# Linear attention and gated linear attention on one core: another order of work in the second pass

## The reference

```
x = x + layernorm(attn(layernorm(x)))      # 16 heads of 32: relu(q), relu(k), linear attention
x = x + layernorm(ffn(layernorm(x)))       # 8 heads of 64: gated linear attention, 5 paths

# inside ffn, per tile of rows
q1, k1, v = x@Wq, x@Wk, x@Wv
q2 = x@Wqa@Wqb;  k2 = softmax(x@Wka@Wkb)
gk1, gk2 = log_sigmoid(x@Wg1a@Wg1b + bg1)/16, log_sigmoid(x@Wg2a@Wg2b + bg2)/16
e = softmax(x@We); one expert of 4 per row (top 1)
o  = chunk_gla(q1, k1, v, gk1) + sum over experts of chunk_gla(q2*e, k2*e, v, gk2*mask)
o  = o * rsqrt(mean(o*o) + eps) * norm_w * silu(x@Wga@Wgb)
return o @ Wo
```

## Time and profile before

| | us |
|---|---|
| median of 3 runs (3140.97 to 3148.92) | 3148.73 |
| the profiled execution | 3142.66 |
| its span, first to last instruction | 3140.8 |
| TensorE busy | 2876.9 (92%) |
| VectorE busy | 1962.6 (62%) |
| ScalarE busy | 1639.7 (52%) |
| GpSimd busy | 1355.5 (43%) |

### The profile page before, as it was taken

How to read it: one execution, slowest core, us unless ns; L and a number is a source line. 1 busy time by engine, 2 the same in 40 slices (tenths; PEclk the granted TensorE clock), 3 DMA queues, 4 the chain that set the end, 5 groups by cost and what they waited for, 6 DMA issues and landing times.

```text
span 3140.8 us, 56322 instructions
## 1 busy us (share of the span) xinstructions
PE 2876.9 (92%) x20720; PEld 1830.1 (58%) x20720; DVE 1962.6 (62%) x3878; ACT 1639.7 (52%) x3281; POOL 1355.5 (43%) x1006
## 2 busy tenths in 40 slices
PE   6999899999999999999879988999999999999997
PEld 3444566666666666666534445666666666666665
DVE  4442666667666676666544426666667666666675
ACT  4332555555555565555433325555556555555553
POOL 2873444444444444444322334444444444444443
PEclk9999999999999999999889999999999999999999
DMA  4121000000000000000021110000000000000000
GB/s 171 61 94 41 18 20 20 20 20 20 20 20 20 20 20 20 20 20 20 18 85 57 67 41 18 20 20 20 20 20 20 20 20 20 20 20 20 20 20 11
DMA packets 48376, 97.49 MB, mean 31 GB/s; under 512 B 5376, under 2 KB 5376, under 8 KB 47680
## 3 DMA queue, kind: packets, MB, share of 16 engines
q1 hardware_dynamic: 37008, 68.44, 6.5%
q10 hardware_dynamic: 9792, 17.83, 1.5%
q0 software_dynamic: 1520, 10.50, 0.8%
HBM read 63.19 MB, written 33.55 MB: 31 GB/s over the span
## 4 chain that ended last, share of the span: by engine, by line
PE 77%; DVE 16%; ACT 3%; issue 3%; POOL 1%; DVEq 0%; DMA 0%; POOLq 0%; SPq 0%; ACTq 0%
PE psum L303 12%; PE psum L448 11%; PE psum L304 11%; PE psum L305 11%; PE psum L547 5%; DVE region L1106 5%; PE psum L437 4%; PE psum L312 4%; PE psum L457 4%; PE psum L413 3%; DVE region L1090 3%; PE psum L353 2%; PE psum L423 2%; ACT ogT L730 2%; PE psum L352 2%
## 5 line engine op out<-in xcount | busy, mean ns | idle before, releaser
L977 POOL TENSOR_TENSOR region<-region,kfac 128x512 f32<-128x512 f32 x64 | 66.8, 1043 | 842.3 <-DVE kfac L1190 842.3
L448 PE MATMUL psum<-region 128*128 128x128 f32 x2560 | 352.2, 305 | 10.8 <-POOL region L959 10.8
L448 PEld LDWEIGHTS psum<-region 128*128 128x128 f32 x2560 | 346.1, 221 | 14.5 <-issue 11.1
L959 POOL TENSOR_TENSOR region<-region,mb 128x512 f32<-128x512 f32 x256 | 322.7, 1292 | 73.3 <-ACT region L620 72.9
L992 POOL TENSOR_TENSOR region<-region,decay 64x1280 f32<-64x1280 f32 x128 | 298.3, 2330 | 117.9 <-DVE decay L1206 112.9
L972 POOL TENSOR_SCALAR region<-region,m 128x512 f32<-128x512 f32 x256 | 172.9, 697 | 285.7 <-DVE hm L1141 210.5
L303 PE MATMUL psum<-wb,region 128*128 128x512 f16 x768 | 292.4, 381 | 3.3 <-DVE mb L1155 3.3
L304 PE MATMUL psum<-wb,region 128*128 128x512 f16 x768 | 292.0, 380 | 0.0
L305 PE MATMUL psum<-wb,region 128*128 128x512 f16 x768 | 291.7, 380 | 0.0
L951 POOL TENSOR_TENSOR region<-region 128x1024 f32<-128x1024 f32 x64 | 146.7, 2292 | 287.4 <-DVE region L1302 229.9
L1302 DVE SCALAR_TENSOR_TENSOR region<-psum,region 128x512 f16<-128x512 f32 x64 | 44.3, 692 | 261.0 <-ACT region L791 261.0
(11 more groups left out here) (233 smaller groups left out, 7580.7 us busy)
## 6 DMA issues: line engine op xcount, KB each, us to landing
region<-x_in SPq DMA_DIRECT2D x128, 256.0 KB, 2.7
q_cols<-region ACTq DMA_DIRECT2D x64, 256.0 KB, 2.4
region<-q_cols SPq DMA_DIRECT2D x64, 256.0 KB, 2.9
out_rows<-region SPq DMA_DIRECT2D x60, 256.0 KB, 2.0
region<-wb_in POOLq DMA_DIRECT2D x1, 3072.0 KB, 11.2
region<-wqkv_in SPq DMA_DIRECT2D x4, 512.0 KB, 6.2
region<-wqkv_in POOLq DMA_DIRECT2D x2, 1024.0 KB, 5.6
region<-wproj_in POOLq DMA_DIRECT2D x2, 1024.0 KB, 7.4
```

Of the source, the lines that this page charges most:

```text
L448: last = mm(bank[7][:, pr * P:(pr + 1) * P], q, state[:, pr, path, :], start=(pr == 0 and path == 0), stop=False, skip_group_check=True)
L959: last = nc.gpsimd.tensor_tensor(qm[:, e, :, :], q2T, mb[:, e, :].unsqueeze(1).to_broadcast([P, PAIRS, P]), ALU.mult)
```

## The change

Nothing is added or removed but one wait; pieces of `step` trade places on three engines. On TensorE `inter` and `intra` of the last tile stand between `project_v` and `gates`; `den` stands behind `project_q`; `out_mm` stands right behind `og_transpose`, ahead of `cumulate`; `half_sums` stands behind `y_mm`. Since `inter` writes bank 7, it now also waits for low0_ok of tile n, after which ScalarE has read the low-rank products. ScalarE and VectorE follow with their own pieces.

```diff
-            def inter(n):
+            def inter(n, front):
                 pe.wait_ge(S("out_ok"), prev(n))
+                if front:
+                    pe.wait_ge(S("low0_ok"), cur(n + 1))
                 pe.wait_ge(S("state_ok"), cur(n))
...
                 if front:
                     low_rank(n)
                     project_v(n)
+                if back:
+                    inter(m, front)
+                    intra(m, mp)
+                if front:
                     gates(n)
                     project_k2(n)
+                    label_bc(n)
+                    project_k(n)
+                    project_q(n)
                 if ahead:
                     den(n + 1, mp)
-                if front:
-                    label_bc(n)
-                if back:
-                    inter(m)
-                    intra(m, mp)
-                if front:
-                    project_k(n)
-                    project_q(n)
                 if back:
                     og_transpose(m)
+                    out_mm(m)
                 if front:
                     cumulate(n)
-                if back:
-                    out_mm(m)
-                if front:
-                    half_sums(n)
                 if ahead:
                     y_mm(n + 1)
                 if front:
+                    half_sums(n)
                     transposes(n)
...
# ScalarE
                     front_v(n, p)
+                    front_router(n)
+                if back:
+                    back_square(m)
+                if front:
                     front_gates(n, 0)
-                    front_router(n)
+                if back:
+                    back_rms(m)
+                if front:
                     front_gates(n, 1)
                     front_ke(n)
+                    front_sig_high(n)
+                    front_sig(n)
                 if ahead:
                     ahead_z(n + 1)
                 if back:
-                    back_square(m)
-                if front:
-                    front_sig_high(n)
-                if back:
-                    back_rms(m)
-                if front:
-                    front_sig(n)
-                if back:
                     back_og(m)
+                    back_norm3(m)
                 if front:
                     front_exps(n)
-                if back:
-                    back_norm3(m)
-                if front:
                     front_exs(n, p)
...
# VectorE
                     front_router(n)
+                if back:
+                    back_norm(m)
+                if front:
                     front_masks(n)
                     front_kmax(n)
                     front_kdiff(n)
-                    front_logsig(n)
-                if ahead:
-                    ahead_qz(n + 1, mp)
-                if back:
-                    back_norm(m)
-                if front:
-                    front_lslow(n)
                 if back:
                     back_normed(m, mp)
                     back_gated(m, mp)
                     back_split(m)
                 if front:
+                    front_logsig(n)
                     front_kfac(n)
+                    front_lslow(n)
                     front_sil(n, p)
                 if ahead:
+                    ahead_qz(n + 1, mp)
                     ahead_qz_split(n + 1)
```

## The result

The changed kernel takes 3356.19 us (median of 4 runs, 3356.14 to 3357.26), the kernel before 3147.64 (4 runs, 3140.97 to 3148.92): a ratio of 1.067, 95% interval 1.065 to 1.069. It is slower, as forecast, but by 209 us and not by 400: 3356 lies under the stated range of 3370 to 3660, and 9 us from the time that the prediction gave to its second rival (3347).

The account below looks back on a forecast made before the run. TensorE was taken as the bound, 77% of the chain of waits. Step 38.7 us, new pauses 8.0, removed 2.85, clock 3.3: 45.2, 6.5 longer; 62 steps give 403, first steps 4, forecast 3550 us, range 3370 to 3660.

Parts of the forecast that it names:

- second rival: New pauses come, but the clock stays up or falls lie inside pauses: step 41.9 us, 3347 in all; chance 0.10.
- What the change removes: TensorE's pause ahead of the gates goes, 2.43 us a step from start to start.
- The four new pauses: Places in a step where TensorE now comes too early: 8.0 us in sum, at full clock.
- (a): Project_k, now right behind the labels, waits for VectorE's masks: 1.65 us a step.
- (b): Project_q waits for ls_ok from VectorE's front_logsig, behind four instructions of the last tile: 3.08 us a step.
- (c): Out_mm waits for ScalarE's copy, behind two activations on den's result: 2.08 us, replacing an old wait of 0.42.
- (d): State products wait for x1, since the half sums behind y hold ScalarE's centring back: 1.2 us a step.
- The clock: TensorE's falls to half clock behind the new pauses, taken as 3.3 us a step, between nothing and 6.
- the lower end: Clock falls after the change cost nothing, as half-speed project_k would lie inside VectorE's 5.67 us.
- The two ends: The first steps of the two batches gain part of the project_q and out_mm pauses: some 2 us each, 4 in all.
- 6 more by the median: Added to the forecast because the profiled execution, 3142.7 us, lay 6 us under the median of the runs, 3148.7.
- The clock's cost before: In the kernel before, the clock's fall behind the gates' pause costs 2.0 us a step: 38.72 against 36.68.

Follow-up runs that it names:

- these three moves: Changed kernel with front_logsig back behind front_kdiff (and back_rms behind Ln), den ahead of the labels, or centring ahead of front_exs: 3243.49, 3327.88, 3304.79 us.
- the new order: Kernel before with TensorE's blocks reordered to give each wait its own cover, ScalarE and VectorE following: 2913.87 us, ratio 0.926.
- the fillers: Matmuls with unread results: ahead of project_k and project_q in the changed kernel, 3331.59 us; ahead of the gates in the kernel before, 3027.17 us.

## Why the prediction was wrong

*What the change removes: right.* The gates' wait is gone from the list.

*The four new pauses: right, none more than 0.2 us off.* Bracketed idle times against the forecast, which counts from start to start, where the 0.17 that the record of the matmul before them hides comes on top:

| pause | forecast | measured (+ 0.17) |
|---|---|---|
| (a) project_k, masks | 1.65 | 1.50 (1.67) |
| (b) project_q, front_logsig | 3.08 | 2.74 (2.91) |
| (c) out_mm, the copy | 2.08 | 1.85 (2.02) |
| (d) state products, x1 | 1.2 | 1.03 (1.2) |

A step at full clock came to 41.43 against 41.9. The queues named as causes are the causes: moving what was held to blame for (b), (c) and (d) shortened that pause at full clock (2.7 to 1.3, 1.85 to 1.12, 1.03 to nothing, of which 0.5 came back at xn_transpose). By themselves these three moves give 113, 28 and 51 us. For (a) no run was made that changes it alone; it is there in the kernel with inter and intra alone moved, and gone in the new order, which puts other work behind the labels. One estimate inside (b) was wrong: "So even VectorE's old order would leave a pause of 2 to 3 us here." It took ScalarE's Ln to be done 7.0 us after the gates' start; it is done after 5.9, and with front_logsig back in its old place, and back_rms behind the Ln, 1.3 us are left.

*The clock: this is the step that failed.* "I take 3.3: (b) and (c) stand for one fall each at about the 1.62 us that the single fall costs." Measured: 41.87 - 41.43 = 0.44 a step, and 24.6 / 62 = 0.40 by the fillers. Two things were wrong in it. The number of falls: there is one a step in 28 of 30 and none in the two others, not two, although three pauses of 1.5 to 2.7 us stand in it. And the price: in 20 steps the fall came behind (a), on project_k, where it cost nothing, in 8 behind (b), on project_q, where it cost 1.7 us, and never behind (c) or (d). The argument for "it costs nothing" (at half speed project_k lies inside VectorE's 5.67 us) stood in the prediction as the lower end, with a chance of 0.10, and the measured cost lies near that end: a fall behind the first pause of a cluster slows work whose successor waits for another engine anyway. Why it comes there so often, and once only, no run tells. With 0.4 in place of 3.3 the sum is 41.9 + 0.4 - 38.7 = 3.6 a step, 223 + 4 us, 3376 by the median. The 20 us that are left come from the step at full clock, 41.43 and not 41.9, which is 29 us; the four pauses explain 0.2 of these 0.47 us a step, the rest is open. The two ends work the other way. (The prediction's own sum with the "6 more by the median" is 3556, not 3550; this changes nothing.)

*The clock's cost before, 2.0 a step: right*, and the fillers show it (36.68, predicted 36.7). So the change gives back 1.6 us a step at the clock and loses 4.75 in pauses (41.43 - 36.68); 62 times the difference is 196.

*The two ends:* the first steps of the batches were to lose 2 us each. From first to second gates they take 39.52 against 30.29, of which 6.25 are inter and intra that now lie between: 3 us each. Some 7 of the 209 us are not accounted for.

*The rivals.* The second came out in time, and nearly in one of its two reasons ("or falls lie inside the pauses"): the falls lie on work that has a pause behind it. The other, that the clock stays up, did not: by the rule of the Trainium skill's page "TensorE: Matmul & The Clock Gate", section "HAM oscillation", no pause here is long enough. Half clock is in 28 of 30 steps of the changed kernel, and in the kernel before it goes when the pause of 2.27 us is filled, so the measurement decides against the rule. The time by that rule, 3347, is near the mark by luck: its step at full clock is 0.47 us too long, and it leaves out the 0.44 that the clock costs.

## What to carry to other kernels

A block that is moved ahead of a wait as its cover may have been the cover of another wait where it came from, as inter and intra were here: before moving it, list what will stand between each producer and its next waiter, on all queues, and put the moved time against each. A fall of TensorE's clock costs most where the slowed work has no wait behind it (1.7 us on project_q, nothing on project_k), so price it by the next wait on the path and not by its length. And when one long pause is left, a small block put into it may be worth more than its length if the clock falls behind the pause (den, 1.0 us long, gave 3.0 a step).

## What the runs showed of the hardware that was not expected

- The same pause doesn't always bring the clock down. Behind 2.27 us it fell in 27 of 30 steps, behind the 1.3 us that den leaves in 1 of 30.
- Filling a pause with matmuls whose result nobody reads cost TensorE nothing in these two kernels (the steps are as long as those at full clock without them, 36.68 and 41.42 us) and gave 3.9% in the kernel before.
- Half clock lasted 3.4 us in each of the changed kernel's steps that had any, but 3.4 or 6.8 us in the kernel before, where the small gates product and fp32 products follow the pause, and 16-bit projections in the changed one. That is not the whole reason: with den back ahead of the labels, five of 30 steps have 6.8 us, and there too 16-bit projections follow the pause. It stays open.
